# A windowed-attention block on one core: narrower weights in the weighed sum, the projection bias added later, and other places for the projections of an image

## The chip, the core and the metric

The kernel runs on one core of a Trainium2 chip. The metric is the device time in microseconds of one execution. Its engines are TensorE (PE; its weight loads are a row of their own, PEld), VectorE (DVE), ScalarE (ACT), GpSimd (POOL) and SyncE (SP), which here only issues DMAs. Each runs its own list of instructions in order, and they wait for one another through semaphores.

## The reference

A block with shifted 8x8 windows on 32 images of 32x32 positions and 64 channels, all in float32: norm, roll by 4, windows, projection to queries, keys and values, attention with 4 heads of 16 channels and a position bias and mask, projection, back to the image, residual, norm, and an MLP of 256 hidden channels.

```python
h = jnp.roll(_ln(x, ln1_g, ln1_b), (-4, -4), axis=(1, 2))
qkv = _window_partition(h, 8) @ qkv_w + qkv_b           # 512 windows, 64 positions
attn = einsum('bnhd,bmhd->bhnm', q, k) * 16 ** -0.5 + bias + mask
out = einsum('bhnm,bmhd->bnhd', softmax(attn), v) @ proj_w + proj_b
x = x + jnp.roll(_window_reverse(out), (4, 4), axis=(1, 2))
return x + jax.nn.gelu(_ln(x, ln2_g, ln2_b) @ fc1_w + fc1_b) @ fc2_w + fc2_b
```

## The kernel before

All of x stays in SBUF: 8 groups of 4 images, a group being 128 partitions (4 images x 32 rows) by 32 columns of 64 channels. A piece is 8 columns, 512 elements on each partition; there are 32 pieces.

**Attention.** An image has two steps (pairs of window rows), so a group has 8 and the kernel PAIRS = 64; step n of an image i is n = 2i or 2i+1. All engines walk the same step numbers, each with its own offset. On PE (L848 to L866), in an odd step: the scores of the next image (`score`, L765), the weighed sum of step n-2 (`weigh`, L802), the tasks of the step, the transposes of the shifted scores of step n-1 (`transpose_probs`, L791), the transposes of the rows of step n-3 (`transpose_o`, L821), then the tasks of step n+0.5. In an even step there are no scores, and the tasks of the step come after the transposes. For one step VectorE (L555 to L566) adds bias and mask to the scores in PSUM and writes them to SBUF (L483), takes the negative maximum (L489) and, three steps behind, divides the weighed sum by the sum of its weights (L496, L498). GpSimd (`shift_pair`, L368) adds the negative maximum (L373). PE transposes the result, ScalarE takes the exponential on the way out of PSUM (L645), and the weighed sum uses it as the weights, with the values and a column of ones as the moving operand of 34 columns.

**Tasks** are written out by hand in `group_tasks` and `all_tasks` (L72 to L93) as (step, kind, which). XT transposes the normed input of the next group (L712), QK makes queries and keys of an image, V its values, Y projects a finished group's attention output, half a group at a time. All use the same two PSUM banks (`work`), so each task waits until the one before it in the list was copied out (BEFORE, L98): XT by L605, QK by L610 and L612, V by L619 in two pieces, Y by VectorE, which adds it to x (L534, L540). The keys are then spread by four SyncE DMAs (`spread_keys`, L277) into kX, double-buffered by image, and `score` waits for these. SyncE's loop (L291 to L299) issues the spreads and the x loads of later groups, 8 DMAs for each group, in order of the steps.

**The first norm** of a group is spread over the steps of the group before it by LN_STEPS (L107): sums and squares' sums on VectorE, mean, centring, power and scaling on GpSimd, squares on ScalarE. `ln_at` (L116) finds what belongs in a step. The last entry of each is for the first four pieces of the second norm.

**The projection bias.** VectorE adds y_bias to x, half a group at a time (`add_y_bias`, L520, 1024 elements), in steps 3 and 5 of each group, once the group is centred; the addition of Y waits for it.

**The MLP** (VectorE L572 to L589, PE L900 to L906) runs over the 32 pieces: VectorE adds the second product to x, sums the piece 4 ahead, scales the piece 2 ahead, sums the squares of the piece 3 ahead, and adds the last bias. GpSimd centres and takes the power, PE transposes, multiplies by w1 and by w2, and ScalarE copies and applies the gelu. A product of float32 operands shows as two loads and two matmuls in the trace.

## Time and profile before

| | |
|---|---|
| median of 3 runs | 501.47 us (500.04 to 504.29) |
| the profiled execution | 500.17 us |
| its span, first to last instruction | 498.4 us |
| PE busy | 436.9 us, 88% |
| VectorE busy | 383.7 us, 77% |
| ScalarE busy | 294.9 us, 59% |
| GpSimd busy | 378.2 us, 76% |
| granted TensorE clock, mean share of full | 0.985 |

Times in the profile are counted from the first instruction of the span. The attention stage begins at some 34 us and its last scores are at 324 us, the MLP's second product runs from 353 to 492 us. In a timeline, a row gives the start of a run of like instructions, its length, and in brackets how long the engine had been idle and what ended that. The starts of two runs show better than a run's length what it costs, since PE's runs overlap at their ends.

### The profile page before, as it was taken

The page shows a single profiled execution, that of the slowest core. Times are in us where ns is not written, and L with a number is a line of the kernel's source. Part 1 is how long each engine was busy: PE and PEld are TensorE (multiplying, and loading weights), DVE is VectorE, ACT ScalarE, POOL GpSimd, SP SyncE. Part 2 cuts the span into 40 slices and gives each one's busy share as a digit, 9 for nine tenths or more (in the row PEclk, how much of TensorE's full clock was granted, in tenths as well). Part 3 has the DMA queues.
Part 4 walks back from the last instruction along what each step waited for, and adds up shares of the span by engine and source line. Part 5 has one row for each costly group of instructions (what it writes and reads, how often), then busy time and mean ns, then how long its engine had stood idle before and what let it go on. Part 6 is the DMA issues. An engine that isn't in the chain of part 4 may idle for free.

```text
span 498.4 us, 21474 instructions
## 1 busy us (share of the span) xinstructions
PE 436.9 (88%) x9630; PEld 329.1 (66%) x9630; DVE 383.7 (77%) x549; ACT 294.9 (59%) x437; POOL 378.2 (76%) x376
## 2 busy tenths in 40 slices
PE   0665978899999899999999999787999999999995
PEld 0542756687777777777777767675566676667664
DVE  2767697889999999899999989965467766777652
ACT  1233665675765665666657646543777677767761
POOL 2658989988988989989889799730588888888830
PEclk9995999999999999999999999999999999999999
DMA  8300523511411511511111101100011321330333
GB/s 166 68 1 22 130 64 69 122 30 26 118 34 26 125 29 24 130 25 27 41 26 35 35 24 31 39 3 3 3 40 49 87 59 30 87 78 11 87 90 81
DMA packets 9986, 27.10 MB, mean 54 GB/s; under 512 B 3368, under 2 KB 3368, under 8 KB 7976
## 3 DMA queue, kind: packets, MB, share of 16 engines
q1 hardware_dynamic: 9896, 25.74, 22.0%
q8 instruction: 76, 1.25, 1.1%
q14 instruction: 14, 0.11, 0.1%
HBM read 9.21 MB, written 8.39 MB: 35 GB/s over the span
## 4 chain that ended last, share of the span: by engine, by line
PE 71%; DMA 9%; ACT 8%; SPq 4%; issue 4%; DVE 2%; ACTq 0%; DVEq 0%
PE work L697 26%; PE outs L697 17%; PE scores L697 16%; DMA kX<-kT 5%; PE scores L798 5%; ACT kT L610 4%; PE scores L838 4%; SPq L283 3%; DMA params<-in_params 2%; ACT qT L612 2%; PE work L712 2%; DMA x<-in_x 1%; PE outs L826 1%; ACT probsT L645 1%; SPq L275 1%
## 5 line engine op out<-in xcount | busy, mean ns | idle before, releaser
L373 POOL TENSOR_TENSOR probs<-probs,negmax 128x1024 f32<-128x1024 f32 x64 | 123.8, 1934 | 27.2 <-DVE negmax L489 27.1
L339 POOL TENSOR_TENSOR stat_rstd<-stat_var,minus_half 128x8 f32<-128x8 f32 (+1 forms) x62 | 104.9, 1691 | 5.0
L483 DVE TENSOR_TENSOR probs<-scores,bias 128x1024 f32<-128x1024 f32 x64 | 77.9, 1217 | 14.2 <-PE scores L697 14.2
L645 ACT ACTIVATE probsT<-scores 128x1024 f32<-128x1024 f32 x64 | 65.6, 1025 | 28.8 <-PE scores L798 28.8
L344 POOL TENSOR_TENSOR xn<-x,stat_mean 128x256 f32<-128x256 f32 (+1 forms) x91 | 78.1, 876 | 4.1
L697 PE MATMUL outs<-vX,probsT 128*64 128x34 f32 x2048 | 72.2, 225 | 9.4 <-issue 8.3
L489 DVE TENSOR_REDUCE negmax<-probs 128x16 f32<-128x1024 f32 x64 | 78.1, 1220 | 2.2
L697 PEld LDWEIGHTS outs<-vX,probsT 128*64 128x64 f32 x2048 | 65.9, 138 | 19.1 <-issue 19.0
L697 PEld LDWEIGHTS work<-params,probs 128*64 128x64 f32 x2048 | 62.3, 138 | 23.5 <-DVE x L577 20.5
L798 PEld LDWEIGHTS scores<-ident,probs 128*128 128x128 f32 x512 | 55.5, 142 | 28.1 <-issue 24.2
L610 ACT ACTIVATE kT<-work,bqkv 128x512 f32<-128x512 f32 x31 | 21.3, 688 | 86.6 <-PE work L697 86.6
L798 PE MATMUL scores<-ident,probs 128*128 128x128 f32 x512 | 70.6, 282 | 1.7 <-issue 1.7
L697 PE MATMUL work<-params,probs 128*64 128x64 f32 x2048 | 66.6, 223 | 0.0
L418 DVE TENSOR_REDUCE stat_sq<-squares 128x8 f32<-128x512 f32 x64 | 43.1, 681 | 28.2 <-ACT squares L597 28.0
L697 PE MATMUL scores<-kX,qT 32*64 32x128 f32 x2048 | 39.5, 282 | 15.6 <-DVE probs L483 5.6
L412 DVE TENSOR_REDUCE stat_sum<-x 128x8 f32<-128x512 f32 x64 | 42.2, 676 | 9.6 <-DMA x<-in_x 9.5
L597 ACT ACTIVATE squares<-xn 128x512 f32<-128x512 f32 x64 | 39.7, 630 | 15.7 <-DVE xn L445 15.3
L682 ACT ACTIVATE probs<-scores,bf 128x1024 f32<-128x1024 f32 x32 | 35.6, 1114 | 20.9 <-PE scores L697 20.8
L336 POOL TENSOR_TENSOR stat_var<-stat_sq,eps 128x8 f32<-128x8 f32 (+1 forms) x62 | 23.2, 375 | 31.6 <-DVE stat_sq L418 31.6
L697 PEld LDWEIGHTS scores<-kX,qT 32*64 32x64 f32 x2048 | 32.0, 133 | 22.5 <-DMA kX<-kT 14.5
L329 POOL TENSOR_TENSOR stat_mean<-stat_sum,one_over_c 128x8 f32<-128x8 f32 (+2 forms) x54 | 17.4, 322 | 33.6 <-DVE stat_sum L412 30.4
L619 ACT ACTIVATE vX<-work 64x512 f32<-64x512 f32 x64 | 39.0, 610 | 4.8 <-PE work L697 4.4
(61 smaller groups left out, 662.4 us busy)
## 6 DMA issues: line engine op xcount, KB each, us to landing
kX<-kT SPq DMA_DIRECT2D x124, 64.0 KB, 2.0
x<-in_x SPq DMA_DIRECT2D x32, 224.0 KB
out<-x SPq DMA_DIRECT2D x28, 224.0 KB
x<-in_x SPq DMA_DIRECT2D x32, 32.0 KB
out<-x SPq DMA_DIRECT2D x28, 32.0 KB
out<-x SPq DMA_DIRECT2D x16, 56.0 KB
params<-in_params SPq DMA_DIRECT2D x1, 805.5 KB, 12.0
out<-x SPq DMA_DIRECT2D x16, 8.0 KB
```

What stands on the lines that cost most here:

```text
L339: nc.gpsimd.tensor_tensor(stat_rstd[:, cols], stat_var[:, cols], minus_half[:, cols], ALU.pow).then_inc(ln_rstd, pieces)
L344: return nc.gpsimd.tensor_tensor(dst, src.rearrange("q (a f) -> q a f", f=C), m, ALU.add)
L373: nc.gpsimd.tensor_tensor(e, e, top, ALU.add).then_inc(shifted, 1)
L412: nc.vector.tensor_reduce(stat_sum[:, r * WIN:(r + 1) * WIN], src.rearrange("q (a f) -> q a f", f=C), AXX, ALU.add, negate=True).then_inc( ...
L418: nc.vector.tensor_reduce(stat_sq[:, r * WIN:(r + 1) * WIN], squares[r % PIECES][:, :].rearrange("q (a f) -> q a f", f=C), AXX, ALU.add).t ...
L483: nc.vector.tensor_tensor(e[:, :].rearrange("q (u a m) -> q a u m", u=2, a=2), scores[k].rearrange("q (a u m) -> q a u m", a=2, u=2), b.re ...
L489: nc.vector.tensor_reduce(negmax[n % 4][:, :], e[:, :].rearrange("q (a m) -> q a m", m=N), AXX, ALU.max, negate=True).then_inc(negmax_read ...
L597: nc.scalar.activation(squares[j % PIECES][:, :], xn[:, j * PIECE:(j + 1) * PIECE], ACT.Square, scale=float(C) ** -0.5).then_inc(ln_square ...
L610: nc.scalar.activation(kT[par][:, :], work[1], ACT.Identity, bias=bqkv[:, 1:2])\
L645: nc.scalar.activation(probsT[n % 2][:, :], trans, ACT.Exp)\
L697: return nc.tensor.matmul(out, lhsT, rhs, start=start, stop=stop)
L798: done = nc.tensor.transpose(trans[:, t * P:(t + 1) * P], probs[n % 4][:, t * P:(t + 1) * P], ident[:, :])
```

## The change

Four things. In `weigh` each product of 64 queries becomes two of 32: the weights are 128x32 and the output goes to 32 partitions, in the order 0, 32, 64, 96. The bias addition leaves its places in the groups; it is made piece by piece (512 elements), the first four in steps 48 to 51, the fifth in step 62, the others in the MLP's rounds on VectorE, and the sum of a piece waits for it instead of the addition of Y. The tasks QK of an image move to even steps, ahead of the weighed sum on PE and ahead of the exponential on ScalarE, an image further ahead of its scores, and V to odd steps, behind the scores and the weighed sum; XT and Y go to the ends of the even steps; the second half of Y is no longer left to the next group. The norm's steps move to one or two steps earlier, and SyncE issues an x load only after the keys of the group's third image have landed.

```diff
@@ group_tasks, all_tasks
-    tasks = [(1, "QK", 2), (1.5, "V", 1), (3, "QK", 3), (3.5, "V", 2), (5.5, "V", 3)]
+    tasks = [(0, "QK", 2), (1, "V", 1), (2, "QK", 3), (3, "V", 2), (5, "V", 3)]
     if not last:
-        tasks += [(2, "XT", 0), (4, "XT", 1), (5, "QK", GI), (7, "QK", GI + 1), (7.5, "V", GI)]
+        tasks += [(6, "QK", GI + 1), (7, "V", GI)]
+        tasks += [(2.5, "XT", 0), (3.5, "XT", 1), (4.5, "QK", GI)] if first else \
+            [(0.5, "XT", 0), (2.5, "XT", 1), (4, "QK", GI)]
     if not first:
-        tasks += [(6.5, "Y", 0)]
+        tasks += [(4.5, "Y", 0), (6.5, "Y", 1)]
...
-        if g >= 2:
-            found.append((STEPS * g + 0.5, "Y", g - 2, 1))
...
-    found.append((PAIRS + 0.5, "Y", GROUPS - 2, 1))
@@ LN_STEPS
-LN_STEPS = {"sum": (-4, -4, -3, -2), "mean": (-4, None, -3, -2), "centre": (-4, -4, -3, -2),
-            "square": (-2, -1, 0, 1), "square_sum": (-1, 0, 1, 2), "rstd": (-1, 0, 1, 2),
-            "scale": (0, 1, 2, 3)}
+LN_STEPS = {"sum": (-5, -5, -4, -4), "mean": (-5, None, -4, -4), "centre": (-5, -5, -4, -4),
+            "square": (-4, -3, -2, -1), "square_sum": (-3, -2, -1, 0), "rstd": (-3, -2, -1, 0),
+            "scale": (-2, -1, 0, 1)}
...
-                  "square": (-1,) * 4, "square_sum": (0,) * 4, "rstd": (0, 0, 1, 1),
+                  "square": (-1,) * 4, "square_sum": (0, 0, 1, 1), "rstd": (0, 0, 1, 1),
...
+Y_BIAS_STEPS = [PAIRS - 2 * STEPS + i for i in range(4)] + [PAIRS - 2]
@@ SyncE
             load(1)
+            load(2)
...
-                if n in (1, STEPS - 2):
-                    load(2 if n == 1 else 3)
-                if g > 0 and s == 2 and g + 3 < GROUPS:
+                if s == 1 and g + 3 < GROUPS:
+                    image = GI * g + 2
+                    sp.wait_ge(kX_loaded[image % 2], 16 * KX_DMAS * ((image + 1) // 2))
                     load(g + 3)
@@ VectorE
                 dve.wait_ge(ln_mean, MEANS + max(s - 3, 0))
+                dve.wait_ge(y_biased, s + 1)
                 row_sum(x[:, s * PIECE:(s + 1) * PIECE], s % PIECES)
-            def add_y_bias(g, half):
-                dve.wait_ge(ln_centred, PIECES * (g + 1))
-                dst = x[:, g * ROW + half * 2 * PIECE:][:, 0:2 * PIECE].rearrange("q (a f) -> q a f", f=C)
-                nc.vector.tensor_tensor(dst, dst, y_bias[:, :].unsqueeze(1).to_broadcast([P, 2 * WIN, C]),
+            def add_y_bias(s):
+                dve.wait_ge(y_added, COUNT["Y", s // PIECES, 1])
+                dst = x[:, s * PIECE:(s + 1) * PIECE].rearrange("q (a f) -> q a f", f=C)
+                nc.vector.tensor_tensor(dst, dst, y_bias[:, :].unsqueeze(1).to_broadcast([P, WIN, C]),
                                         ALU.add).then_inc(y_biased, 1)
...
-                dve.wait_ge(y_biased, 2 * (of + 1))
...
-                if n < PAIRS and n % STEPS in (3, 5):
-                    add_y_bias(n // STEPS, (n % STEPS - 3) // 2)
+                if n in Y_BIAS_STEPS:
+                    add_y_bias(Y_BIAS_STEPS.index(n))
...
                 if s + 4 < S:
                     sum2(s + 4)
+                if s + 5 < S:
+                    add_y_bias(s + 5)
@@ ScalarE
                 squares_of(n)
-                if n % 2:
-                    for kind, of, i in tasks_at(n):
-                        take(kind, of, i)
+                for kind, of, i in tasks_at(n):
+                    take(kind, of, i)
...
-                if n % 2 == 0:
-                    for kind, of, i in tasks_at(n):
-                        take(kind, of, i)
@@ PE, weigh
-                        for w in range(2):
-                            at = (u * HEADS + h) * P + (w ^ k) * N
+                        for rows in range(0, P, 32):
+                            w = rows // N
+                            at = (u * HEADS + h) * P + (w ^ k) * N + rows % N
                             row = (w * 4 + 2 * k + u) * HEADS + h
-                            out = outs[w * N:(w + 1) * N, u * HEADS * VW:(u + 1) * HEADS * VW]\
+                            out = outs[rows:rows + 32, u * HEADS * VW:(u + 1) * HEADS * VW]\
                                 .rearrange("q (p h d) -> q p h d", p=2, h=HEADS)[:, :, h]
-                            done = mm(out, probsT[n % 2][:, at:at + N], vX[image % 2][:, row, :])
+                            done = mm(out, probsT[n % 2][:, at:at + 32], vX[image % 2][:, row, :])
@@ PE, the loop over the steps
                     score((n + 1) // 2)
+                if n % 2 == 0:
+                    for kind, of, i in tasks_at(n):
+                        fill(kind, of, i)
                 if 0 <= n - PV < PAIRS:
                     weigh(n - PV)
...
-                if n % 2 == 0:
-                    for kind, of, i in tasks_at(n):
-                        fill(kind, of, i)
                 for kind, of, i in tasks_at(n + 0.5):
                     fill(kind, of, i)
```

## Rows read from the trace of the kernel before

**Rows 1.** The profile page: the span and the engines' busy time.

```profile
span 498.4 us, 21474 instructions
PE 436.9 (88%) x9630; PEld 329.1 (66%) x9630; DVE 383.7 (77%) x549; ACT 294.9 (59%) x437; POOL 378.2 (76%) x376
```

**Rows 2.** Stretches: start:end, length, busy us of each engine, clock, DMA share, GB/s.

```profile
112.00:324.00 212.00, 196.69 (x5127) 157.30 (x5124) 194.93 (x264) 133.57 (x217) 185.90 (x171) 1.00 0.19 47
353.00:488.00 135.00, 135.00 (x2280) 91.27 (x2276) 90.81 (x143) 95.43 (x118) 102.67 (x108) 1.00 0.24 59
```

**Rows 3.** Timeline of weight loads (start, length): scores of images 1 and 31.

```profile
44.03 1.64 PEld L697 LDWEIGHTS scores<-kX,qT 32*64 32x64 f32 x64 [6.48 <-DMA kX<-kT]
...
323.71 0.97 PEld L697 LDWEIGHTS scores<-kX,qT 32*64 32x64 f32 x64 [1.50 <-DMA kX<-kT]
```

**Rows 4.** Timeline of weight loads in one image.

```profile
212.96 0.98 PEld L697 LDWEIGHTS scores<-kX,qT 32*64 32x64 f32 x64 [0.33 <-issue]
214.11 1.01 PEld L697 LDWEIGHTS outs<-vX,probsT 128*64 128x64 f32 x32 [0.17 <-issue]
215.17 0.21 PEld L697 LDWEIGHTS work<-xT,wqkv 64*64 64x64 f32 x8
216.19 0.86 PEld L798 LDWEIGHTS scores<-ident,probs 128*128 128x128 f32 x8 [0.81 <-issue]
...
217.64 0.56 PEld L697 LDWEIGHTS work<-wqkv,xT 64*64 64x64 f32 x32 [0.38 <-ACT qT L612]
218.57 1.04 PEld L697 LDWEIGHTS outs<-vX,probsT 128*64 128x64 f32 x32 [0.37 <-issue]
219.66 0.86 PEld L798 LDWEIGHTS scores<-ident,probs 128*128 128x128 f32 x8
...
220.90 1.02 PEld L697 LDWEIGHTS work<-params,oT 64*64 64x64 f32 x64 [0.17 <-issue]
221.99 0.97 PEld L697 LDWEIGHTS scores<-kX,qT 32*64 32x64 f32 x64
```

**Rows 5.** Timeline of ScalarE in the same image.

```profile
216.91 0.68 ACT L612 ACTIVATE qT<-work,bqkv 128x512 f32<-128x512 f32 x1
217.48 1.02 ACT L645 ACTIVATE probsT<-scores 128x1024 f32<-128x1024 f32 x1
...
218.65 0.59 ACT L619 ACTIVATE vX<-work 64x512 f32<-64x512 f32 x1
```

**Rows 6.** Waits over the span: us in total, times, longest.

```profile
PEld scores L697 <- DMA kX<-kT: 14.5, 12, 6.5
```

**Rows 7.** Timeline of weight loads in the MLP: the second product, two rounds.

```profile
389.55 1.95 PEld L697 LDWEIGHTS work<-params,probs 128*64 128x64 f32 x64 [0.76 <-DVE x L577]
391.57 0.42 PEld L838 LDWEIGHTS scores<-ident,xn 128*128 128x128 f32 x4
...
394.07 0.26 PEld L697 LDWEIGHTS work<-params,probs 128*64 128x64 f32 x6 [0.76 <-DVE x L577]
```

**Rows 8.** Timeline of weight loads at the start; each product has one moving column.

```profile
17.37 0.55 PEld L697 LDWEIGHTS scores<-params 128*128 128x128 f32 x2
17.80 0.55 PEld L697 LDWEIGHTS scores<-params,ident 128*128 128x128 f32 x2
```

**Rows 9.** VectorE: bias addition from 111.8 to 323.7 us (busy, mean ns | idle); timeline.

```profile
L524 DVE TENSOR_TENSOR x<-x,y_bias 128x1024 f32<-128x1024 f32 x12 | 18.6, 1550 | 0.0
...
214.90 1.21 DVE L483 TENSOR_TENSOR probs<-scores,bias 128x1024 f32<-128x1024 f32 x1
...
217.91 0.68 DVE L412 TENSOR_REDUCE stat_sum<-x 128x8 f32<-128x512 f32 x1
218.50 1.22 DVE L483 TENSOR_TENSOR probs<-scores,bias 128x1024 f32<-128x1024 f32 x1
```

**Rows 10.** Timeline of VectorE in a round of the MLP.

```profile
388.77 0.68 DVE L412 TENSOR_REDUCE stat_sum<-x 128x8 f32<-128x512 f32 x1
390.07 0.69 DVE L426 TENSOR_TENSOR xn<-xn,stat_rstd 128x512 f32<-128x512 f32 x1 [0.63 <-POOL stat_rstd L339]
```

## The prediction

> **What bounds the kernel now.** The page first: over a span of 498.4 us TensorE is busy 88%, VectorE 77%, GpSimd 76% [rows 1]. An average over two stages says little, so I cut the span. In the attention stage, 112 to 324 us, PE is busy 196.69 of 212 us, VectorE 194.93, GpSimd 185.90, at granted clock 1.00; in the MLP stage, 353 to 488 us, PE is busy all 135 us and VectorE 90.81 [rows 2]. So the attention stage has three nearly full engines and the MLP stage one.
>
> Next, the length of one image. The score bursts of images 1 and 31 start at 44.03 and 323.71 us [rows 3]: 30 periods in 279.68 us, 9.32 each. The load queue inside one undisturbed image shows what fills it [rows 4]: scores 212.96, weighed sum 214.11, queries and keys 215.17, transposes 216.19, values 217.64, weighed sum 218.57, transposes 219.66, projection 220.90, next scores 221.99. The starts are 9.03 apart. Real waits are few: values wait 0.38 for the copy of the queries, and the second weighed sum starts 0.93 after values whose burst lasts 0.56 to 0.69, because its exponential is late. ScalarE shows why: it copies the queries from 216.91 and only then takes the exponential, at 217.48 for 1.02 [rows 5]. The rest of the 9.32 is irregular: score bursts wait 14.5 us in all for the keys' DMA, 12 times, the first of 6.5 us at start-up [rows 6].
>
> **The weighed sum.** Before, 16 products a step, 32 loads of 64 columns; after, 32 products and 64 loads of 32 columns, so 2048 more loads and as many more matmuls in the kernel. No row shows a 32-column weight; the nearest bound it. Leaving 0.14 us for the last load's own length, 32 loads of 128x64 take 1.01 us [rows 4], that is 28 ns each with 34 moving columns; in the MLP's second product 64 loads take 1.95 us, 28.7 ns each with 64 moving columns [rows 7]. Twice the moving columns, same pace: the weights set it. With 64-row weights (values, 32 in 0.56) it is 13.5 ns, with 32-row weights and 128 moving columns (scores, 64 in 0.98) 13.3 ns. Multiplied by the tiles that fit the array (2, 4, 8): 57, 55 and 107 ns for each tile. The transposes, one tile of 128 columns, are 103 ns apart. At the start 128-column weights with a single moving column follow each other at 213 ns, two per 0.43 us [rows 8]. So a tile's time is set by the wider of weight and moving operand, and grows with it. At 32 weight columns and 34 moving ones it should be about 33 ns, and with 4 tiles 8 ns per load: 64 x 8 = 0.53 us, and 0.67 to the next burst where it is now 1.06. The ends: 0.4 us (free of any floor) and, if a narrower weight costs as much as a wide one and nothing more overlaps, 64 x 29 = 1.86. I take 0.67, w below, since every row that varies tile width moves that way.
>
> The 57 ns for 34 and for 64 moving columns could also be a floor. Then four tiles give 14.3 ns per load, 0.91 us: no change. The Trainium skill's page "TensorEngine Tiling (Array Packing)", section Instruction Overhead, says just this: about 60 cycles per matmul, and one should not take the tiling factor from a dimension that is already small. By that page this part would bring nothing; it is the second case below.
>
> **Order of an image on PE.** After: scores, weighed sum, values, transposes; then queries and keys, weighed sum, transposes, projection or input transposes. From [rows 4]: scores to weighed sum 1.15; w; values 0.66; then queries and keys wait until ScalarE has copied the values (two pieces of 0.59 [rows 5], 1.3 with what lies around them), which covers the 1.07 of transposes (216.19 to 217.64, less 0.38 idle); queries and keys to the next weighed sum 1.08, where the exponential, now behind the values' copy, is just ready; w; transposes, projection and the wait for its exponential 2.33 (219.66 to 221.99). Sum 6.52 + 2w: 8.64 with the old w of 1.06, 7.86 with the new one.
>
> **Keys an image ahead.** Before, copy, spread and landing of the keys had from the product's burst at 215.17 to the scores at 221.99 [rows 4], and an x load could intrude. After, a further image of PE work, 8 us, lies between, and the x load is issued only when the second next image's keys have landed. SyncE's queue: the wait stands ahead of 8 loads, and behind them is the spread of the next keys, which has that image to spare. I cost the queue at nothing and take the kX waits after start-up as gone; the first 6.5 us stays. If that cover fails the waits return, 8 us at most.
>
> **VectorE.** In the stage of 23 images it is busy 194.93 us: 8.47 an image. Of this the bias addition is 12 x 1.55 = 18.6 us, 0.81 an image [rows 9]; without it 7.66. But its load is uneven: bias, maximum and division take 3.0 a step (214.90 to 217.91), a sum 0.6 [rows 9], and after the change one image has two sums and an output addition and square sum (8.95) and the next the same addition and squares (8.5), the other two 6.6 and 7.2. The excess over 7.86 delays the first bias addition of the next image, and the transposes now follow only 1.15 + w + 0.66 after the score start, the very time that this addition ends. So the lag of about 1.1 and 0.85 shows once each per group, less half covered: 0.4 an image. Forecast period 7.86 + 0.4 = 8.25.
>
> **GpSimd** is busy 185.90 / 23 = 8.1 us an image and its work does not change. Its steps are uneven too, but a shifted score is transposed on PE an image after its scores were made, with four buffers between, so a lag of a few us stays hidden. Just: at 8.25 it is 98% full. The two steps by which the norm moves forward follow the move of the input transposes and leave its distance to them as it was: nothing.
>
> **ScalarE** has 133.57 / 23 = 5.8 us an image; only its order counts, above.
>
> **MLP.** 27 bias additions of 512 elements come in (5 more lie in light attention steps), each an operation on 512 elements like the sum there, 0.60 from start to start as in [rows 9]. VectorE's round has the sum at 388.77, then 0.63 idle until the scale at 390.07, which GpSimd's power releases [rows 10]. The new one fits that gap: 389.37 to 390.05. PE's round of 4.52 (389.55 to 394.07 [rows 7]) transposes the scaled piece at 391.57, 0.8 after the scale ends. Cost nothing; without that cover 27 x 0.6 = 16 us.
>
> **Sum.** 30 periods of 8.25 are 247.5, and I keep 3 us for the first group's slow clock and start: 250.5 instead of 279.7, less 29.2. Behind the last scores three weighed sums shorten by 0.39 each, and one projection burst of 1.09 leaves there, having stood partly behind an exponential, 0.6: less 1.8. Start-up to 44 us and MLP 0. 498.4 - 31 = 467.4, and the profiled execution's time was 1.8 above its span: 469. That execution, 500.17, is 1.3 below the median 501.47, so I say 470.
>
> **Rivals.**
> 1. Forecast: w 0.67, 470 us. Chance 0.60.
> 2. The floor: w stays 0.95 to 1.06. Period 8.64 and a lag of 0.1, 8.75: 30 x 8.75 + 3 = 265.5, tail 0.6: 498.4 - 14.8 + 1.8 + 1.3 = 487; with the smaller w, 480. For it: equal pace at 34 and 64 columns. Against it: 213 ns at one moving column. Chance 0.18.
> 3. Another engine binds: GpSimd at 98%, or lags that add up, period 8.7: 484. For it: three engines are above 87% in [rows 2]. Chance 0.10.
> 4. The bias addition shows in the MLP's round, 16 us: 486. Against it: 0.63 idle and 0.8 spare. Chance 0.04.
> 5. Slower: narrow weights don't overlap and keep their 29 ns; the burst is 1.86 and w 2.0. Period 6.52 + 4.0 = 10.5: 30 x 10.5 + 3 = 318, 38 more, with 3 in the tail: 498.4 + 41 + 1.8 + 1.3 = 543. It turns into a loss once w passes about 1.4 us, 20 ns per load. For it: no row shows four column tiles at once. Against it: values and scores run in more tiles faster. Chance 0.06.
> The rest, 0.02, is no change to speak of: the order makes new waits as large as those removed.
>
> **Numbers.** Time 470. Range: down to 463 (the period falls to GpSimd's 8.1 and none of the 3 us is left) and up to 487, which takes in the rivals 2 to 4. One per cent, 5 us, is about what can be told from no change. Faster by more: 0.92; within: 0.02; slower: 0.06.
>
> **What would show it.** Weighed-sum bursts of 64 loads in about 0.5 us; a distance of 0.66 and 1.3 around values; score starts 8.2 apart, longer after the two heavy images; no kX wait after start-up; VectorE's idle before the MLP scale near zero and the MLP round still 4.52. A burst near 0.9 is the second case, beyond 1.3 the fifth. The forecast is wrong if PE then waits mostly for the shifted scores of GpSimd, or if the faster bursts are held back by something no row shows, such as the pace at which 128 instructions reach the array in 0.5 us.

## The result, and the profile after

The changed kernel takes 525.02 us (median of 4 runs, 516.66 to 529.54) where the kernel before, on the same chip, takes 500.75 (4 runs, 496.42 to 504.29). The ratio is 1.0408, 95% interval 1.0216 to 1.06: slower, against a forecast of 470. (The ratios here leave disturbed executions out, two of these four and the profiled one of h1_shifted_by_half among them, so they need not be the quotient of the medians.) A second measurement, e1_after_again, gave 1.0405 (1.0336 to 1.0474). The profiled execution took 516.66 us and is the fastest of the four.

The page of the changed kernel, to be held against [rows 1]; the last row is the queue that brings instructions (packets, MB, share of the DMA engines):

```profile
span 514.9 us, 25612 instructions
PE 428.0 (83%) x11678; PEld 313.8 (61%) x11678; DVE 385.6 (75%) x565; ACT 297.9 (58%) x437; POOL 371.9 (72%) x376
...
q8 instruction: 92, 1.51, 1.2%
```

The same row in the kernel before:

```profile
q8 instruction: 76, 1.25, 1.1%
```

PE's busy time falls by 8.9 us, that of the others grows by 3.0 at most, and yet the span grows by 16.5 us. No engine became the bound; the time is idle time of all of them.

Stretches of the changed kernel (start:end, length, busy us of PE, its loads, VectorE, ScalarE, GpSimd, then clock, DMA share, GB/s): the scores of image 1 to those of image 31, the stretch of [rows 2], and 135 us of the MLP:

```profile
43.30:342.20 298.90, 249.40 (x8428) 191.73 (x8429) 235.34 (x325) 175.73 (x278) 240.82 (x228) 0.95 0.21 48
112.00:324.00 212.00, 176.76 (x6039) 135.00 (x6027) 169.27 (x236) 124.44 (x198) 168.56 (x160) 0.97 0.19 45
371.00:506.00 135.00, 135.00 (x2282) 91.22 (x2280) 105.78 (x168) 95.52 (x118) 102.73 (x108) 1.00 0.24 59
```

The loss is all in the attention stage. Its 30 periods take 298.9 us (9.96 each) instead of 279.7 ([rows 3]). PE is busy 249.4 of them, and no engine is busy over 84%, where three had been above 87% [rows 2]. What follows the last scores takes 172.7 us instead of 174.7.

Weight loads of the changed kernel in an image and a half (start, length, what, how many, in brackets the idle time before and what ended it), to be held against [rows 4]:

```profile
218.19 0.54 PEld L699 LDWEIGHTS work<-params,oT 64*64 64x64 f32 x28 [1.04 <-issue]
218.81 0.96 PEld L699 LDWEIGHTS scores<-kX,qT 32*64 32x64 f32 x64
219.94 0.40 PEld L699 LDWEIGHTS outs<-vX,probsT 128*32 128x32 f32 x35 [0.17 <-issue]
221.95 0.34 PEld L699 LDWEIGHTS outs<-vX,probsT 128*32 128x32 f32 x29 [1.61 <-issue]
222.34 0.56 PEld L699 LDWEIGHTS work<-wqkv,xT 64*64 64x64 f32 x32
222.97 0.86 PEld L800 LDWEIGHTS scores<-ident,probs 128*128 128x128 f32 x8
223.79 0.25 PEld L829 LDWEIGHTS outs<-ident,o_rows 128*128 128x128 f32 x2
224.39 0.21 PEld L699 LDWEIGHTS work<-xT,wqkv 64*64 64x64 f32 x8 [0.35 <-ACT vX L625]
225.46 0.67 PEld L699 LDWEIGHTS outs<-vX,probsT 128*32 128x32 f32 x64 [0.86 <-issue]
226.18 0.85 PEld L800 LDWEIGHTS scores<-ident,probs 128*128 128x128 f32 x8
227.00 0.25 PEld L829 LDWEIGHTS outs<-ident,o_rows 128*128 128x128 f32 x2
227.42 1.02 PEld L699 LDWEIGHTS work<-params,oT 64*64 64x64 f32 x64 [0.17 <-ACT qT L618]
228.51 1.00 PEld L699 LDWEIGHTS scores<-kX,qT 32*64 32x64 f32 x64
229.68 0.65 PEld L699 LDWEIGHTS outs<-vX,probsT 128*32 128x32 f32 x64 [0.17 <-issue]
230.38 0.56 PEld L699 LDWEIGHTS work<-wqkv,xT 64*64 64x64 f32 x32
231.79 0.20 PEld L800 LDWEIGHTS scores<-ident,probs 128*128 128x128 f32 x2 [0.86 <-issue]
232.59 0.14 PEld L800 LDWEIGHTS scores<-ident,probs 128*128 128x128 f32 x1 [0.60 <-issue]
```

The narrow burst is as short as hoped: 64 loads in 0.65 us at 229.68, 0.70 to the next burst. But the one at 219.94 stops after 35 of its 64 loads and goes on 1.61 us later; the projection burst before it stopped in the same way at 218.19, and the transposes at 232.59. Nothing is waited for ("issue"): the semaphore of a burst was passed at its first product, and the operands are those of the burst. And the stops have a spacing. From 218.19 to 221.95 lie 28 + 64 + 35 = 127 loads and as many matmuls, 254 instructions; from 221.95 to 232.59 lie 379 loads, 758 instructions, close to three times that (the waits between bursts, instructions too, make up the rest). Numbered in the order of PE's program, waits included, every one of the 26 stops of over 0.6 us that no semaphore explains lies at number 200 or 201 modulo 256, whatever product stands there. They take 43.5 us in all (pause of the loads, start to start). In the kernel before, two such stops take 3.0.

What happens at each 256th instruction shows in the DMA queue. In the stretch from 219.5 to 220.7 us, between the stops at 218.19 and 221.95, there is one packet of the instruction queue. This row rounds it to 0.02 MB; it is 16 KB, 1.51 MB over 92 packets:

```profile
q8 instruction: 1, 0.02, 5.5%
```

It runs from 219.60 to 220.65, and the next instructions of PE start at 221.95. That holds throughout: each block of 256 instructions brings one such packet of 0.9 to 1.5 us. I read this as a fetch of instructions; which instructions a packet holds the trace doesn't say. At a stop PE runs on 1.2 to 1.6 us behind the packet's end in nearly every case (median 1.4, never under 1.1), and 2.15 us or more behind its start. And in the changed kernel the packet mostly starts only 1.1 to 1.4 us after the block did. The two together, 1.1 and 2.2 us, make some 3.3 us: a block that PE could use up in less mostly ends in a stop, unless a packet came early, as it does behind slow blocks. That sum does not cover every stop. Seven of the 26, with 13.4 of the 43.5 us, end blocks of 3.4 to 5.1 us whose packet started only 2.9 to 4.0 us after the block. An image now has 576 PE instructions, 2.25 blocks; before it had 448.

PE's waits in the changed kernel, from 43.3 to 342.2 us (total, times, longest), with [rows 6] in view:

```profile
PEld outs L699 <- issue: 53.2, 70, 2.4
PEld work L699 <- issue: 19.5, 24, 2.2
PEld scores L699 <- issue: 16.5, 25, 2.9
...
PEld scores L699 <- DMA kX<-kT: 3.1, 1, 3.1
```

and of the kernel before over the whole span, for the first row:

```profile
PEld outs L697 <- issue: 34.0, 124, 1.2
```

The keys' waits are gone after start-up. In their place stands "issue", with a longest of 2.4 to 2.9 us.

A second loss rides on the first. Four stretches of the changed kernel, columns as above: a long stop, what follows it, and once more:

```profile
53.50:56.00 2.50, 0.27 (x30) 0.15 (x18) 2.17 (x2) 0.00 (x0) 2.50 (x3) 1.00 0.54 99
56.70:60.00 3.30, 3.30 (x34) 3.18 (x27) 3.27 (x5) 2.13 (x3) 3.22 (x5) 0.50 0.06 11
167.80:170.80 3.00, 0.38 (x21) 0.14 (x6) 0.00 (x0) 0.31 (x1) 1.75 (x3) 1.00 0.36 82
172.80:176.00 3.20, 3.20 (x18) 2.15 (x18) 3.17 (x6) 2.44 (x5) 2.07 (x2) 0.50 0.00 0
```

PE stands still for 2.5 or 3 us, and shortly after works at the lower of its two clock levels (0.50, 1.2 GHz). Of seven such falls between 50 and 342 us, six begin 0.5 to 2 us after a stop of over 2.0 us; one such stop, at 252.09, has no fall behind it. In the stretch of the 30 periods PE spends 27.0 us at the lower level; before it was 6.0, all at the start.

VectorE in a round of the MLP, as in [rows 10]:

```profile
405.87 0.68 DVE L529 TENSOR_TENSOR x<-x,y_bias 128x512 f32<-128x512 f32 x1
406.58 0.69 DVE L430 TENSOR_TENSOR xn<-xn,stat_rstd 128x512 f32<-128x512 f32 x1
407.99 0.69 DVE L422 TENSOR_REDUCE stat_sq<-squares 128x8 f32<-128x512 f32 x1 [0.72 <-ACT squares L603]
```

The bias addition fills the former gap in front of the scaling, and PE's round stays 4.52 us.

### The profile page after: what moved, and what is told of

It is laid out like the page before. It is cut to its first block, busy times and chain, and to the rows that moved or that the text cites. A ratio compares the mean times of both kernels' runs of the same rounds, so it can differ in the third digit from the quotient of the medians.

```text
span 514.9 us, 25612 instructions
## 1 busy us (share of the span) xinstructions
PE 428.0 (83%) x11678; PEld 313.8 (61%) x11678; DVE 385.6 (75%) x565; ACT 297.9 (58%) x437; POOL 371.9 (72%) x376
## 3 DMA queue, kind: packets, MB, share of 16 engines
q8 instruction: 92, 1.51, 1.2%
## 4 chain that ended last, share of the span: by engine, by line
PE 77%; issue 10%; ACT 5%; DVE 3%; DMA 3%; SPq 1%; DVEq 0%
PE work L699 27%; PE scores L699 16%; PE outs L699 15%; PE scores L800 11%; PE scores L841 4%; ACT vX L625 3%; PE work L714 3%; DMA params<-in_params 2%; PE outs L829 2%; ACT probsT L651 1%; DVE probs L487 1%; SPq L277 0%; DVE x L538 0%; DVE negmax L493 0%; DMA kX<-kT 0%
## 5 line engine op out<-in xcount | busy, mean ns | idle before, releaser
L377 POOL TENSOR_TENSOR probs<-probs,negmax 128x1024 f32<-128x1024 f32 x64 | 121.8, 1904 | 51.0 <-DVE negmax L493 50.9
L487 DVE TENSOR_TENSOR probs<-scores,bias 128x1024 f32<-128x1024 f32 x64 | 78.0, 1218 | 31.4 <-PE scores L699 31.2
L699 PEld LDWEIGHTS outs<-vX,probsT 128*32 128x32 f32 x4096 | 44.1, 110 | 58.3 <-issue 57.3
L800 PE MATMUL scores<-ident,probs 128*128 128x128 f32 x512 | 74.2, 290 | 3.4 <-issue 2.4
L699 PE MATMUL outs<-vX,probsT 128*32 128x34 f32 x4096 | 52.3, 199 | 24.9 <-issue 20.6
L800 PEld LDWEIGHTS scores<-ident,probs 128*128 128x128 f32 x512 | 58.0, 146 | 8.0 <-issue 5.0
L422 DVE TENSOR_REDUCE stat_sq<-squares 128x8 f32<-128x512 f32 x64 | 43.2, 681 | 25.3 <-ACT squares L603 25.2
L699 PE MATMUL scores<-kX,qT 32*64 32x128 f32 x2048 | 42.1, 283 | 13.7 <-issue 5.2
L603 ACT ACTIVATE squares<-xn 128x512 f32<-128x512 f32 x64 | 39.6, 628 | 15.8 <-DVE xn L449 15.8
L699 PEld LDWEIGHTS scores<-kX,qT 32*64 32x64 f32 x2048 | 33.0, 133 | 23.0 <-issue 16.5
L699 PE MATMUL work<-xT,wqkv 64*64 64x512 f32 x256 | 41.0, 703 | 5.4 <-ACT qT L618 1.4
L699 PE MATMUL scores<-xT,w 64*128 64x512 f32 x128 | 36.1, 641 | 1.7 <-DVE x L544 1.7
```

The costliest lines, as they stand in the source:

```text
L377: nc.gpsimd.tensor_tensor(e, e, top, ALU.add).then_inc(shifted, 1)
L422: nc.vector.tensor_reduce(stat_sq[:, r * WIN:(r + 1) * WIN], squares[r % PIECES][:, :].rearrange("q (a f) -> q a f", f=C), AXX, ALU.add).t ...
L487: nc.vector.tensor_tensor(e[:, :].rearrange("q (u a m) -> q a u m", u=2, a=2), scores[k].rearrange("q (a u m) -> q a u m", a=2, u=2), b.re ...
L603: nc.scalar.activation(squares[j % PIECES][:, :], xn[:, j * PIECE:(j + 1) * PIECE], ACT.Square, scale=float(C) ** -0.5).then_inc(ln_square ...
L699: return nc.tensor.matmul(out, lhsT, rhs, start=start, stop=stop)
L800: done = nc.tensor.transpose(trans[:, t * P:(t + 1) * P], probs[n % 4][:, t * P:(t + 1) * P], ident[:, :])
```

## The experiments

Two theories were to be told apart. **Supply**: the new products are as fast as wanted, but PE uses up its instructions faster than they are brought. **Form**: the 32-column products, four column tiles one after the other, make PE stop by themselves. The prediction's own theory (three nearly full engines and the order decide) was carried along. Ratios are to the kernel before on the same chip, with 95% intervals; "stops" are those of over 0.6 us at a block's edge in the 30 periods of the profiled execution.

| run | us | ratio | period | stops | us in them |
|---|---|---|---|---|---|
| before | 500.75 | | 9.32 | 2 | 3.0 |
| after | 525.02 | 1.0408 (1.0216 to 1.06) | 9.96 | 26 | 43.5 |
| e1_after_again | 519.53 | 1.0405 (1.0336 to 1.0474) | 10.03 | 28 | 46.1 |
| e2_wide_weights | 499.29 | 1.0016 (0.9983 to 1.005) | 9.26 | 10 | 10.5 |
| e3_only_narrow | 510.39 | 1.0229 (1.0167 to 1.029) | 9.73 | 15 | 25.2 |
| e4_narrow_odd_steps | 512.49 | 1.0278 (1.0201 to 1.0354) | 9.75 | 20 | 31.9 |
| f1_spread_wide | 494.62 | 0.988 (0.9842 to 0.9919) | 9.13 | 0 | 0 |
| f2_spread_narrow | 505.55 | 1.0062 (1.0022 to 1.0103) | 9.55 | 26 | 31.3 |
| f3_padded | 539.1 | 1.0758 (1.0705 to 1.0811) | 10.63 | 16 | 21.7 |
| f4_bias_only | 504.77 | 1.0095 (1.0053 to 1.0136) | 9.47 | 2 | 2.9 |
| g1_spread_old_bias | 499.72 | 0.9959 (0.9927 to 0.9991) | 9.29 | 0 | 0 |
| g2_order_only | 506.82 | 1.0098 (1.0066 to 1.013) | 9.51 | 13 | 14.5 |
| g3_narrow_half | 495.5 | 0.9876 (0.9826 to 0.9926) | 9.11 | 21 | 31.4 |
| g4_spread_wide_again | 495.2 | 0.9871 (0.983 to 0.9913) | 9.17 | 1 | 0.9 |
| h1_shifted_by_half | 524.78 | 1.0385 (1.0282 to 1.0489) | 10.04 | 32 | 49.2 |
| h2_narrow_quarter | 478.71 | 0.9545 (0.9467 to 0.9623) | 8.67 | 8 | 13.6 |

**e1_after_again.** The changed kernel, unchanged.

> The changed kernel once more, for comparison on the same chip. Supply theory: PE's instructions come in blocks of 256 (16 KB), one transfer each, and a block that is used up before the next has come leaves PE standing inside a burst; 2.25 blocks an image here. Again 515 to 530 us, some 25 to 30 breaks of over 0.6 us inside bursts, all at the same place modulo 256 in PE's program. If the breaks came from waits or from DMA traffic, their places would differ from one run to the next.

The same loss, and 25 of the 26 stops at the same instruction again. The length of a stop varies (3.75 us where it was 2.47, at number 968), its place hardly. The link from a long stop to the clock is looser here: the five falls of the clock all begin inside a stop of 1.96 us or more or within 1 us of its end, but three of the five stops of over 2.0 us (2.48, 2.10, 2.31) have none.

**e2_wide_weights.** The change without the narrow products.

```diff
-                        for rows in range(0, P, 32):
+                        for w in range(2):
...
-                            done = mm(out, probsT[n % 2][:, at:at + 32], vX[image % 2][:, row, :])
+                            done = mm(out, probsT[n % 2][:, at:at + N], vX[image % 2][:, row, :])
```

> The whole change but for the weighed sum, which keeps its 16 products of 64 queries. Supply theory: 1.75 blocks an image as before the change, period 8.7, 480 to 487 us, at most 5 breaks inside bursts. Rival, the new order of the tasks makes the loss: 510 us or more and over 15 breaks. Rival, each part is worth little: about 500.

The time is missed by 12 us. Images without a stop are 8.68 us long, as forecast for the order with wide weights, but there are ten stops although the weights are wide. Weight loads of e2_wide_weights:

```profile
105.13 1.08 PEld L699 LDWEIGHTS work<-params,oT 64*64 64x64 f32 x64 [0.17 <-issue]
106.28 1.03 PEld L699 LDWEIGHTS scores<-kX,qT 32*64 32x64 f32 x64
107.49 1.01 PEld L699 LDWEIGHTS outs<-vX,probsT 128*64 128x64 f32 x32 [0.17 <-issue]
108.55 0.48 PEld L699 LDWEIGHTS work<-wqkv,xT 64*64 64x64 f32 x25
110.12 0.20 PEld L699 LDWEIGHTS work<-wqkv,xT 64*64 64x64 f32 x7 [1.10 <-issue]
```

The new order puts the values behind the weighed sum, so four small-product bursts follow each other without a pause: 64 + 64 + 32 + 32 loads, 384 instructions, in 4.0 us. In the order before it was 320 in a row, and then queries and keys with their long products [rows 4]. So the order's gain is paid back by the supply, and what the changed kernel loses comes with the narrow products: e1 against e2, measured on one chip, is 20.2 us.

**e3_only_narrow.** The kernel before, with the narrow products alone.

> The kernel before, with only the weighed sum in 32 products of 32 queries. Supply theory: 2.25 blocks an image, over 15 breaks inside bursts, slower than before, 505 to 525 us. Rival, order: the shorter bursts save 0.3 us a step, 485 to 495 us, breaks as few as before (2).

As the supply theory had it: 1.0229. The worst stop, in its weight loads:

```profile
79.22 0.24 PEld L697 LDWEIGHTS outs<-vX,probsT 128*32 128x32 f32 x13 [3.71 <-issue]
```

An image without a stop takes as little as 8.30 us here: the narrow products save their 0.35 us twice an image and lose it again.

**e4_narrow_odd_steps.** The changed kernel, narrow products in odd steps only.

```diff
-                        for rows in range(0, P, 32):
+                        for rows in range(0, P, 32 if k else N):
```

> The change with narrow weights in odd steps alone: 2.0 blocks an image. Supply theory: between wide and narrow and nearer to wide, as blocks last 4.1 us on average: 485 to 500 us, 5 to 15 breaks. If the order is the cause: as the changed kernel, over 510. If narrow weights alone did harm in proportion: half way between e2 and e1.

Missed: 512.49, above the range, with 20 stops for the expected 5 to 15. Of the three expectations the last comes nearest, harm in proportion to the narrow products: half way between e2 and e1 is 509.4. Half of the added instructions bring more than half of the stops' time (31.9 us, between e2's 10.5 and e1's 46.1). By its time this run does not speak for supply against form.

**f1_spread_wide** and **f2_spread_narrow.** The order made with the supply in mind: queries and keys, eight long products, go into odd steps between the scores and the weighed sum, an image further ahead, and the values to even steps. f1 has wide weights, f2 narrow ones.

```diff
-    tasks = [(0, "QK", 2), (1, "V", 1), (2, "QK", 3), (3, "V", 2), (5, "V", 3)]
+    tasks = [(1, "QK", 3), (2, "V", 1), (4, "V", 2), (6, "V", 3)]
...
-                    image = GI * g + 2
+                    image = GI * g + 3
...
-                if n % 2 == 0:
-                    for kind, of, i in tasks_at(n):
-                        fill(kind, of, i)
+                for kind, of, i in tasks_at(n):
+                    fill(kind, of, i)
...
```

> e2 (wide weights, bias in the MLP) with queries and keys in odd steps between the scores and the weighed sum, two images ahead, and values at the start of even steps: the slow burst of 8 long products stands between the dense ones. Same 452 or so PE instructions an image. Supply theory, in its form that a break comes when some 200 instructions behind the request are used up in under about 3.4 us: at most 4 breaks, period 8.6 to 8.8, 478 to 486 us. Rival, the number of instructions alone decides: breaks as in e2 (10), 496 to 500. Rival, the tasks' order has hidden waits of its own: over 500.

> f1 with 32-query weights, 2.25 blocks an image as the changed kernel. By density: fewer breaks than e1's 28, 8 to 20, and 485 to 505 us, under the changed kernel but no gain over f1, as blocks last 3.5 us at a period of 7.9. By number alone: 515 or more.

f1 has not one stop, with the same 448 PE instructions an image as e2, and is the first version faster than the kernel before, by 1.2%. Weight loads of f1_spread_wide:

```profile
224.67 0.99 PEld L699 LDWEIGHTS scores<-kX,qT 32*64 32x64 f32 x64 [0.33 <-issue]
225.83 0.21 PEld L699 LDWEIGHTS work<-xT,wqkv 64*64 64x64 f32 x8 [0.17 <-ACT xT L611]
226.84 1.01 PEld L699 LDWEIGHTS outs<-vX,probsT 128*64 128x64 f32 x32 [0.81 <-issue]
227.90 0.86 PEld L800 LDWEIGHTS scores<-ident,probs 128*128 128x128 f32 x8
...
229.15 0.56 PEld L699 LDWEIGHTS work<-wqkv,xT 64*64 64x64 f32 x32 [0.17 <-issue]
230.13 1.04 PEld L699 LDWEIGHTS outs<-vX,probsT 128*64 128x64 f32 x32 [0.43 <-issue]
```

Behind the 64 loads of the scores stand 8 whose matmuls run for 1 us, and the stretch breaks up. It missed its 478 to 486 all the same: periods are 8.81 to 9.20, because the weighed sum still waits 0.43 for its exponential and queries and keys wait up to 0.6 for VectorE's addition of Y. In f2 the narrow products bring the stops back, 26 of them, shorter than in the changed kernel (1.2 us on average for 1.7), and the gain of the order goes into them: 505.55, half a microsecond above the range, and more stops than the 8 to 20 expected.

**f3_padded.** e2_wide_weights with 16 tiny products more (32 columns by 2) in front of each weighed sum: as many PE instructions as in the changed kernel, and the real products wide.

```diff
+                for j in range(16):
+                    mm(outs[32 * (j % 4):32 * (j % 4) + 32, 300:302], ident[:, 0:32], ident[:, 0:2])
```

> e2 with 16 products of 32 columns of the identity by 2 columns, into unused PSUM columns, ahead of each weighed sum: the weights that do the work stay wide, the number of instructions is that of the changed kernel. They cost PE some 0.3 to 0.4 us a step themselves, which makes 18 us. Supply theory: over 15 breaks, 515 us or more. Rival, it is the narrow form of the real products (their PSUM writes or weights' reads) that halts PE: breaks as in e2, 10 or fewer, about 510 to 517. The breaks decide.

539.1 us, 1.0758. The 32 loads of the padding take 0.35 us a step, 0.7 an image, 21 us in all; the other 19 us against e2 come with stops (11.2 us more) and the clock (27.3 us at the lower level for 5.9, at most 11 us of loss). It speaks for supply but less cleanly than it should, since the padding is itself of 32 columns.

**f4_bias_only.** The kernel before with the bias addition in the MLP as in the change.

> The kernel before with only the projection bias moved to the MLP's rounds. If VectorE had been a bound in the attention stage: 490 or less. My sum by PE's waits, whose 9.0 us an image hold no wait for VectorE: 495 to 499, that is a gain of 0 to 4. MLP round 4.52 as before in either case; if the addition shows there, 5.1 and over 510.

Missed: 504.77, not 495 to 499, and 1% slower than the kernel before. Relieving VectorE by 0.8 us an image gives nothing in the order before: images without a stop or a wait for keys last 8.96 us with and without the relief, so PE's order sets the period there. Its profiled execution shows two long images, of 13.4 and 11.9 us. The first has a supply stop (1.64 us idle) at 134.02 and the second an idle time of PE of 2.01 us before the transposes at 274.28, and at each the clock falls; the stretch has 15.8 us at the lower level for 6.0, at most 5 us of loss. The second idle time comes from the moved additions. Timeline of f4_bias_only there:

```profile
271.46 1.04 POOL L353 TENSOR_TENSOR xn<-xn,stat_rstd 128x512 f32<-128x512 f32 x1
271.62 1.43 DVE L527 TENSOR_TENSOR x<-x,y_bias 128x512 f32<-128x512 f32 x1
...
272.97 1.21 DVE L486 TENSOR_TENSOR probs<-scores,bias 128x1024 f32<-128x1024 f32 x1
...
274.28 1.09 PE L802 MATMUL scores<-ident,probs 128*128 128x128 f32 x4 [2.01 <-issue]
```

One addition placed in steps 48 to 51 holds VectorE for 1.43 us, where it takes 0.68 in the MLP; the addition of bias and mask behind it ends only at 274.18, and the transposes, which wait until these scores have been taken, follow. The five additions in steps 48 to 62 are slow because of GpSimd, as it seems: in f4, in f1 and in the changed kernel each of them (0.80 to 2.28 us) begins while GpSimd works on `probs` or `xn` and ends 0.55 us after that operation does. The same steps cost f1 some 2.3 us: its images there take 10.05 and 9.89 us, where those of the group before take 8.82 and 8.93.

**g1_spread_old_bias**, **g2_order_only**, **g4_spread_wide_again.** f1, and e2, with the bias addition back in the groups; and f1 again.

```diff
-                if n in Y_BIAS_STEPS:
-                    add_y_bias(Y_BIAS_STEPS.index(n))
+                if n < PAIRS and n % STEPS in (3, 5):
+                    add_y_bias(n // STEPS, (n % STEPS - 3) // 2)
...
```

> The spread order with the 64-column weighed sum, as in f1_spread_wide, but with the bias addition back in steps 3 and 5 of each group (half a group at a time, and the addition of Y waiting for it, as before). If the order alone brought the gain of f1, this gives 489 to 496 us, no break of over 0.6 us at a block's edge, and the MLP's round stays 4.52. If taking 18.6 us of bias additions out of the attention stage was what let the order pay, it gives 498 us or more and VectorE's lag shows in front of the transposes.

> The change's order of tasks, norm steps and x loads alone: 64-column weighed sum, bias addition in the groups. The supply theory says about what e2_wide_weights gave, 496 to 503 us, with some 10 breaks of over 0.6 us at block edges and an undisturbed image of 8.7 to 9.0 us. The prediction's theory (three full engines, bias relief worth 0.8 us an image on VectorE) says the relief counts: 505 us or more, with images of 9.0 to 9.5 us that have no break.

> f1_spread_wide a second time, on the chip of this call: 491 to 497 us, a ratio of 0.98 to 0.995 to the kernel before, no break of over 0.6 us at a block's edge.

f1 holds (0.9871). Without the bias relief it is 499.72, and g2 506.82 where e2 was 499.29. By the ratios, moving the bias is worth some 4 us (0.8 to 0.9%) in either new order, and in the old one it gained nothing. Both came out where the relief was said to count; g2's stops (13, 14.5 us) are those of the supply. The order of the change alone, without its other two parts, loses 1%.

**g3_narrow_half** and **h2_narrow_quarter.** The changed kernel, but from step 2 on the weighed sum leaves out two of the four heads, or three.

```diff
-                    for h in range(HEADS):
+                    for h in range(HEADS if n < 2 else 2):
```

> The changed kernel, but from step 2 on the weighed sum computes heads 0 and 1 only: 16 products of 32 queries, 32 loads and 32 matmuls a step, as many instructions as before, each of the new form. Half of the heads is left out. If the number of PE instructions decides (448 an image again, though used up faster), most of the long stops go: at most 15 breaks of over 0.6 us, 465 to 490 us. If the narrow form itself, four column tiles one after the other, made PE stop, at least 20 breaks stay and the time is 500 us or more. The floor theory is excluded already; the burst should be 0.32 to 0.40 us.

> The changed kernel, but from step 2 on the weighed sum computes head 0 alone: 8 products of 32 queries, 16 loads and 16 matmuls a step, 384 PE instructions an image. Three quarters of the heads are left out. If the narrow form is what stops PE, the eight products a step still do: over 10 breaks of over 0.6 us. If the pace of use decides, blocks last longer: at most 10 breaks with 10 us in all, 470 to 490 us. In either case a break begins its new block 1.2 to 1.7 us after an instruction fetch has ended.

g3, with 448 PE instructions an image again, kept 21 stops at 495.5 us. Its time lies between the two expectations, its stops are as many as the form theory wanted (at least 20), so by itself it speaks rather for form. It shows that the count alone is not the rule: the image also got shorter, and a narrow burst uses 64 instructions in 0.38 us. Nine of its stops, 16.8 us, are also of the kind whose packet started late, over 2.6 us after the block. With 384 an image (h2) 8 stops are left and 478.7 us, both as the supply theory expected, but with 13.6 us in the stops for at most 10. One of them, weight loads of h2_narrow_quarter:

```profile
222.73 0.42 PEld L699 LDWEIGHTS work<-wqkv,xT 64*64 64x64 f32 x18
224.99 0.47 PEld L699 LDWEIGHTS work<-wqkv,xT 64*64 64x64 f32 x14 [1.84 <-issue]
```

It sits among the values' products, 64 columns wide.

**h1_shifted_by_half.** The changed kernel with 128 PE instructions more at the start of the program, outside the stretch.

```diff
             mm(outs[:, 0:C], v_bias[0:C, :], proj[0:C, :]).then_inc(y_bias_summed, 1)
+            for j in range(32):
+                mm(trans[32 * (j % 4):32 * (j % 4) + 32, 0:2], ident[:, 0:32], ident[:, 0:2])
```

> The changed kernel with 32 tiny products (128 instructions) more on PE at the start, at some 17 us, and nothing else: the edges of the 256-instruction blocks fall half a block earlier in the work. Supply theory: all breaks of over 0.6 us move with them, to the same position (200 or 201 of 256) in the new count, so none is at the product at which the changed kernel had one; some 20 to 32 of them, 512 to 535 us. Rival (the breaks belong to certain bursts, their form or their banks): they stay at the same products of the same images, positions 72 and 73 in the new count.

This decides it. The products are those of the changed kernel, and only their numbers differ. All 32 stops stand at number 200 or 201 modulo 256 in the new count, so none is at a product at which the changed kernel had one. Weight loads of h1_shifted_by_half:

```profile
220.40 0.40 PEld L699 LDWEIGHTS outs<-vX,probsT 128*32 128x32 f32 x33
222.93 0.34 PEld L699 LDWEIGHTS outs<-vX,probsT 128*32 128x32 f32 x28 [2.13 <-issue]
```

The form theory has no room for that, nor for the stops in the values' products of e2.

## Why the prediction was wrong

**The step that failed** is the one headed "The weighed sum". It priced 2048 more loads and as many more matmuls by their time in the array, 8 ns each, and gave their supply no term. The last sentence of the prediction named "the pace at which 128 instructions reach the array in 0.5 us" as something no row shows; it had neither a price nor a chance. The price was 43.5 us in stops for 3.0, against some 21 us that the narrow products save. Rows that hinted at it were there: the instruction queue's 76 packets, and two unexplained stops in the kernel before. The fifth rival had the right sign with the wrong mechanism: the narrow loads do overlap.

**The array's time itself was right.** w was forecast at 0.67 and is 0.70 to 0.72. The loads follow at (0.70 - 0.14) / 64 = 8.8 ns, 35 ns for a tile of 32 columns; 33 was the estimate. The second rival, a floor, is refuted. One premise of the estimate is doubtful: the 213 ns of [rows 8], held against the floor, is close to the 196 ns at which transposes, also with 128 weight columns, follow each other at the lower clock level (8 in 1.57 us, f3), and the trace has no record of the clock there. The Trainium skill, page "TensorEngine Tiling (Array Packing)", section Instruction Overhead, has one moving column cost as much as 60 and advises against tiling a dimension that is already small; this trace does not bear that out for 34 moving columns, since the burst fell from 1.01 to 0.65 us.

**The order of an image** was right in its parts: scores to weighed sum 1.17 (forecast 1.15), values 0.63 (0.66), the wait for their copy 1.42 (1.3), queries and keys to weighed sum 1.07 (1.08), and weighed sum to next scores, less the burst, 2.33 as forecast. Images without a stop are 7.95 to 8.03 us long, forecast 7.86 plus a lag that averages 0.4. Whether VectorE's lag and GpSimd's 8.1 us would show can't be judged: stops of 1 to 3 us give both time to catch up.

**The order has a cost that the step left out**: it joins four bursts of small products, and by e2 that costs ten stops with wide weights, 10.5 us, where the second rival's sum had 14.2 to gain.

**The keys**: right, no wait after start-up. **The bias in the MLP**: right, the round stays 4.52. The five additions left in the attention stage were called light and priced at nothing; they take 8.1 us instead of 3.4, and by f1 and f4 PE can wait for them. **The tail**: 2.0 us shorter, forecast 1.8. But that the relief of VectorE is worth something by itself was wrong by f4, and right with a new order by f1 against g1 and e2 against g2.

**The sum.** Without its stops the stretch is 298.9 - 43.5 = 255.4 us; forecast were 250.5. The clock may account for the rest: 21 us more at half speed cost at most 10. The forecast span of 467.4 with the stops added is 510.9; it is 514.9. These are numbers of the fastest of the four executions; what made the others up to 13 us longer no profile shows.

**Open.** Why a fetch mostly starts 1.1 to 1.4 us after the start of a block, and sometimes 3 to 4 us after it, no run explains. That decides between a stop and none in blocks that last 4 to 6 us, and it may be why half the added instructions (e4) cost more than half the loss. There is a lead. In the changed kernel seven blocks begin inside the values' burst. Six of them have 16 to 35 loads before PE's next wait, that of the queries and keys for the values' copy, and their packet starts 3.8 to 4.2 us after the block. The seventh has 42 loads before that wait, and its packet starts at 1.0 us. So a wait soon behind a block's start may delay the fetch; no run moved a wait to find out. Nor did a run change the DMA traffic beside the instruction packets. That the clock falls because of the stops is likely: f1, g1 and g4, with no stop or one of 0.9 us, have no fall in the stretch after their start-up, and elsewhere the falls stand at stops or other idle times of PE. Three have no supply stop before them, but PE idle for 2.01 us (f4, at 274.28), 1.73 us (g3, at 266.09) and 2.33 us (h2, at 254.62), so the idle time may be what counts, whatever its reason. No run changed stops and clock apart.

## What to carry to other kernels

Beside the time of each engine stands the supply of its instructions: count them per unit of time, and look for bursts of short ones that follow each other. Splitting products to use the array better halves the work in each instruction; where 256 of them are used up in under some 3.3 us, long products placed between the bursts (f1, 0.988, of which the moved bias is 0.8%) are worth more than a faster burst (e3, 1.0229). An unexplained "issue" in the middle of a burst, at a fixed spacing in instructions, is the sign to look for.

## What the hardware showed that was not expected

- PE's program comes in blocks of 256 instructions, one packet of 16 KB each, 0.9 to 1.5 us long in the changed kernel and up to 1.75 in the others. At a stop the next block starts 1.2 to 1.6 us after the packet's end in nearly every case, in all fourteen profiled executions that have such stops; never under 1.1.
- Four column tiles of 32 columns overlap: 64 loads with their matmuls of 34 columns in 0.65 us.
- Falls of TensorE's clock to the 1.2 GHz level stand at long stops: six of seven in the changed kernel begin 0.5 to 2 us after one of over 2.0 us, all five in e1_after_again inside or within 1 us of one of 1.96 us or more. Not every such stop brings one: in e1 three of five of over 2.0 us did not. At that level 8 transposes take 1.57 us (f3) instead of 0.86.
- An addition of 128x512 on VectorE, with both operands and the result in SBUF, takes 0.68 us in the MLP, beside GpSimd's small 128x8 operations, and up to 2.28 us when it begins while GpSimd works on 128x1024 or 128x512 elements: it then ends 0.55 us after that operation (all five such additions of the attention stage in the changed kernel, in f1 and in f4).
- A stop of 3.0 us at one place was 1.6 in another execution of the same kernel: the places repeat, the lengths do not.
